# Last two attention units of the second batch split by ACT and DVE, and the fourth feed-forward chunk in pieces between the last tiles

## The reference

```python
x = hidden                                    # (2, 1024, 512)
n = layernorm(x)
q, k, v = n @ q_w.T + q_b, n @ k_w.T + k_b, n @ v_w.T + v_b      # 16 heads of 32
attn = softmax(causal(q @ k.T / sqrt(32))) @ v
x = x + layernorm(attn @ o_w.T + o_b)
h = silu(layernorm(x) @ w_gate.T) * (layernorm(x) @ w_up.T)      # 2048 wide
x = x + layernorm(h @ w_down.T)
```

## Time and profile before

| | |
|---|---|
| median of 3 runs | 1028.7 us (1028.31 to 1029.04) |
| the profiled execution, its own time | 1027.8 us |
| its span from first to last instruction | 1026.0 us |
| mean granted clock of TensorE | 0.986 of full speed |
| busy: PE, DVE, POOL, ACT | 980.4, 720.4, 691.2, 410.4 us |
| start and projections of the first batch | 0 to about 85 us |
| units 14 and 15 | 444.7 to 471.4 and 471.4 to 500.1 us |
| residual of the second batch | 500 to 554.4 us |

### The profile page before, as it was taken

The page is one execution under the profiler, slowest core; times in us unless marked ns, Lnnn a source line. Parts: engine busy times, 40 slices in busy tenths (PEclk is TensorE's granted clock), DMA queues, the critical chain, the costliest instruction groups (busy, mean ns, idle before and its releaser), DMA issues.

```text
span 1026.0 us, 15720 instructions
## 1 busy us (share of the span) xinstructions
PE 980.4 (96%) x5669; PEld 754.7 (74%) x5669; DVE 720.4 (70%) x1418; ACT 410.4 (40%) x717; POOL 691.2 (67%) x498
## 2 busy tenths in 40 slices
PE   5998999999999999998898999999999999999997
PEld 4766676766776776755576888888888888888886
DVE  6676777887597777875778577776665877777722
ACT  4215455555215555554335233332543433333232
POOL 4204888799535999999266976653688768776273
PEclk8999999999999999999899999999999999999999
DMA  6232333323421333231132222111432322211043
GB/s 224 78 88 58 96 83 89 87 76 78 134 82 35 93 88 89 73 95 42 62 112 96 93 76 77 62 62 44 161 113 93 112 77 74 98 62 62 20 154 134
DMA packets 49182, 90.70 MB, mean 88 GB/s; under 512 B 10448, under 2 KB 10960, under 8 KB 48848
## 3 DMA queue, kind: packets, MB, share of 16 engines
q1 hardware_dynamic: 48560, 89.43, 28.7%
q10 hardware_dynamic: 544, 0.26, 0.1%
HBM read 55.84 MB, written 8.39 MB: 63 GB/s over the span
## 4 chain that ended last, share of the span: by engine, by line
PE 75%; DVE 11%; POOL 7%; ACT 2%; issue 2%; DMA 2%; SPq 1%; POOLq 0%; ACTq 0%; DVEq 0%
PE ps L1649 19%; PE ps L1651 18%; PE ps L1650 18%; PE ps L1744 6%; PE ps L1715 5%; PE ps L1778 5%; POOL p_sum L747 3%; PE ps L1792 1%; DVE p_sum L1268 1%; DVE xt_lo L1282 1%; DMA x_in<-x 1%; POOL p_sum L743 1%; POOL p_sum L740 1%; DVE stats L1444 1%; PE ps L1752 1%
## 5 line engine op out<-in xcount | busy, mean ns | idle before, releaser
L1305 DVE CUSTOM_DVE_ANT_0 ps<-ps,mask_q 128x384 f32<-128x384 f32 (+7 forms) x256 | 189.9, 780 | 67.9 <-PE ps L1715 65.0
L1744 PE MATMUL ps<-q_stack,k_stack 98*128 98x512 f32 (+3 forms) x384 | 117.0, 382 | 9.4 <-ACT p_own L982 3.3
L1715 PE MATMUL ps<-k_stack,q_stack 96*128 96x512 f32 (+3 forms) x384 | 108.9, 364 | 1.6 <-DVE m_full L1305 0.9
L769 POOL TENSOR_TENSOR dn_lo<-dn_raw,dn_hi 128x512 fp32r<-128x512 f32 x48 | 65.7, 1370 | 47.2 <-ACT dn_hi L1074 47.2
L1744 PEld LDWEIGHTS ps<-q_stack,k_stack 98*128 98x128 f32 x384 | 62.7, 192 | 33.7 <-ACT p_own L982 8.3
L1715 PEld LDWEIGHTS ps<-k_stack,q_stack 96*128 96x128 f32 x384 | 66.6, 192 | 27.1 <-DVE m_full L1305 11.4
L814 POOL TENSOR_TENSOR gu_lo<-s_raw,gu_hi 128x1024 fp32r<-128x1024 f32 x27 | 64.8, 2402 | 23.2 <-ACT gu_hi L1145 23.2
L982 ACT ACTIVATE p_own<-ps 128x512 f32<-128x512 f32 x112 | 61.0, 598 | 42.8 <-PE ps L1744 23.7
L982 ACT ACTIVATE x_in<-ps 128x512 f32<-128x512 f32 x112 | 60.9, 598 | 36.5 <-PE ps L1744 20.4
L1168 ACT ACTIVATE silu<-ps 128x512 f32<-128x512 f32 x27 | 16.2, 599 | 141.5 <-DVE ps L1540 141.5
L810 POOL TENSOR_TENSOR a_lo<-gu_raw,a_hi 128x512 fp32r<-128x512 f32 x27 | 35.8, 1327 | 51.8 <-ACT a_hi L1138 51.7
(11 more groups left out here) (224 smaller groups left out, 2827.8 us busy)
## 6 DMA issues: line engine op xcount, KB each, us to landing
gu_raw<-gu_w SPq DMA_DIRECT2D x37, 512.0 KB, 3.6
dn_raw<-dn_w SPq DMA_DIRECT2D x48, 256.0 KB, 2.6
x_in<-x SPq DMA_DIRECT2D x32, 256.0 KB, 4.4
q_stack<-st_hi SPq DMA_DIRECT2D x128, 64.0 KB, 2.0
k_stack<-st_hi SPq DMA_DIRECT2D x128, 64.0 KB, 2.0
qk_raw<-qk_w SPq DMA_DIRECT2D x16, 256.0 KB, 3.0
q_stack<-st_lo SPq DMA_DIRECT2D x64, 64.0 KB, 2.0
k_stack<-st_lo SPq DMA_DIRECT2D x64, 64.0 KB, 2.0
```

The source lines that it names most:

```text
L769: nc.gpsimd.tensor_tensor(dn_lo[:, s], dn_raw[:, s], dn_hi[:, s].bitcast(F32), ALU.subtract).then_inc(dn_split, 1)
L1305: nc.vector.tensor_tensor_reduce(out=scores, in0=scores, in1=mask_q[:, SEQ - (t + 1) * P:], scale=1.0, scalar=MASKED, op0=ALU.add, op1=ALU ...
L1715: last = nc.tensor.matmul(bank[:, 0:width], q_stack[0:QK_ROWS, s, h, t * P:(t + 1) * P], k_stack[0:QK_ROWS, s, h, half * CH:half * CH + wi ...
L1744: last = nc.tensor.matmul(bank[:, at_col:at_col + n * P], k_stack[0:ROWS, s, h, kt * P:(kt + 1) * P], q_stack[0:ROWS, s, h, t * P:(t + n) ...
```

## The change

Units 14 and 15: quarters 0, 1 and 2 of `attn` are rounded by ACT between the rounds of unit 14 (after rounds 0, 4 and 6) and their rests are taken by DVE, quarter 0 in unit 14 before its last four maxima, quarters 1 and 2 in unit 15 before the adds. POOL's three splits go; its eighth token step moves behind the second residual tile. DVE's adds of unit 15 begin before `normalise(14)`, which stands between the third and the fourth. PE does the late products of the unit before first, then four unread products, the transposed maxima, and five (unit 14) or ten (unit 15) more. Start: seven unread products instead of four before tiles 1 to 7. Residual: chunk 3 is cut into its gate part after T 5, and halves of its up part after T 6 and T 7; there are no unread products before T 6 and three before T 7. ACT rounds tile 6 earlier and puts tile 7 between the two silus; DVE's `hidden(0)` comes before tile 7's rest. `down(0)` waits bank by bank, behind ten unread products.

```diff
-BUSY_AT_TILE = {**{_t: 4 for _t in range(1, TT)}, 13: 6, 2 * TT + 14: 8, 2 * TT + 15: 8}
+BUSY_AT_TILE = {**{_t: 7 for _t in range(1, TT)}, 13: 6, 2 * TT + 15: 3}
+HI_OF_PARTS = (0, 4, 6)
-AFTER_TILE = {("O", 3): 1, ("T", 4): 2, ("T", TT - 1): 3}
+WHOLE = ((0, 0, KT), (1, 0, KT))
+AFTER_TILE = {("O", 3): (1, WHOLE), ("T", 4): (2, WHOLE), ("T", 5): (3, ((0, 0, KT),)), ("T", 6): (3, ((1, 0, KT // 2),)),
+              ("T", 7): (3, ((1, KT // 2, KT),))}
@@ POOL, units @@
-                    if u >= UNITS - 2:
+                    if b + 1 < BATCH and u >= UNITS - 2:
                         pool.wait_ge(late_full, late_of((b + 1) * UNITS - 1, 1))
                         split_attn(b, u - (UNITS - 2))
                     if g + 1 == ALL_UNITS:
                         gu_rest(0)
                         gu_rest(1)
-                        of_tokens(T_STEPS - 1)
...
-                split_attn(b, KT - 2)
+                if b + 1 < BATCH:
+                    split_attn(b, KT - 2)
@@ POOL, residual tiles @@
+                    if b + 1 == BATCH and t == 1:
+                        of_tokens(T_STEPS - 1)
@@ ACT @@
+            def hi_of_part(b, k):
+
+                act.wait_ge(late_full, late_of((b + 1) * UNITS - 1, 1))
+                act.wait_ge(bank_free, use_of_sums(b * UNITS + 2 * k + 1) + 2)
+                nc.scalar.activation(xt_hi[:, b, k, :], attn[:, k, :], ACT.Copy).then_inc(attn_part_hi, 1)
...
+                    if g + 2 == ALL_UNITS and r in HI_OF_PARTS:
+                        hi_of_part(BATCH - 1, HI_OF_PARTS.index(r))
...
-                    if t >= lag:
+                    if t >= lag and (b + 1 < BATCH or t <= TT):
                         hi_of_xt(b, t - lag, use_of("T", b, t - lag))
+                    if b + 1 == BATCH and t == TT:
+                        hi_of_xt(b, t + 1 - lag, use_of("T", b, t + 1 - lag))
...
-                    for n in range(PARKED):
-                        silus(n)
+                    silus(0)
+                    hi_of_xt(BATCH - 1, TT - 1, use_of("T", BATCH - 1, TT - 1))
+                    silus(1)
@@ DVE @@
-            def add_up(g):
+            def add_up(g, between):
...
+                between()
                 vec.wait_ge(p_ready, scored(g, 4, 1))
...
+            def lo_of_part(b, k):
+
+                vec.wait_ge(attn_part_hi, k + 1)
+                nc.vector.tensor_tensor(xt_lo[:, b, k, :], attn[:, k, :], xt_hi[:, b, k, :].bitcast(F32), ALU.subtract).then_inc(attn_split, 1)
...
                 max_rows(g)
+                if not ahead:
+                    for k in range(1, KT - 1):
+                        lo_of_part(BATCH - 1, k)
...
-                if has_sums(g):
+                if not ahead:
+                    vec.wait_ge(bank_full, use_of_sums(g - 1) + SUM_BANKS)
+                    add_up(g, lambda: normalise(g - 1, None))
+                elif has_sums(g):
                     normalise(g - 1, None)
-                if not ahead:
-                    add_up(g)
                 if ahead:
                     maxima(g + 1, range(EARLY, len(MAXES) - 4))
+                if ahead and not projected:
+                    lo_of_part(BATCH - 1, 0)
...
+                    if b + 1 == BATCH and t == TT + 2:
+                        hidden(0)
                     if t >= lag:
                         lo_of_xt(b, t - lag, use_of("T", b, t - lag))
+                    if b + 1 == BATCH and t == TT + 2:
+                        hidden(1)
...
-                    if b + 1 == BATCH and t > TT:
-                        hidden(t - TT - 1)
@@ PE @@
-                if g + 2 == ALL_UNITS + 1 and n == EARLY:
-                    keep_busy(LATE_BANK, 5)
+                if g + 1 == ALL_UNITS and n == EARLY:
+                    keep_busy(LATE_BANK, 4)
...
             def transpose_maxima(g):
 
-                if g + 2 >= ALL_UNITS:
-                    pe.wait_ge(late_free, late_of(ALL_UNITS - 1, 1))
-                    keep_busy(LATE_BANK, 10)
...
-                transpose_maxima(g)
+                if projected:
+                    transpose_maxima(g)
                 if has_sums(g):
                     values(g - 1, LATE_VALUES)
+                if not projected:
+                    pe.wait_ge(late_free, late_of(ALL_UNITS - 1, 1))
+                    keep_busy(LATE_BANK, 4)
+                    transpose_maxima(g)
+                    keep_busy(LATE_BANK, 10 if g + 1 == ALL_UNITS else 5)
...
-            def gate_and_up(n):
+            def gate_and_up(n, pieces=WHOLE):
...
-                for part, bank in enumerate((0, 2) if blk else (G_BANK, U_BANK)):
+                for part, k0, k1 in pieces:
+                    bank = (0, 2)[part] if blk else (G_BANK, U_BANK)[part]
...
-                    last.then_inc(gu_full, 1)
+                    if k1 == KT:
+                        last.then_inc(gu_full, 1)
@@ PE, down @@
+                if n == 0:
+                    pe.wait_ge(bank_free, USES - (USES - 1 - banks[0]) % RING)
+                    keep_busy(banks[0], 10)
...
                 for t in range(BT):
+                    if n == 0:
+                        pe.wait_ge(bank_free, USES - (USES - 1 - banks[t]) % RING)
...
-            pe.wait_ge(bank_free, USES)
             down(0, first=True)
```

More of the change, by code:

```diff
@@ L451, in build @@
         attn_last_split = sem("attn_last_split")
+        attn_part_hi = sem("attn_part_hi")
         var_ready = sem("var_ready")
@@ L1853, in residual @@
                     extra(kind, t)
-            def gate_and_up(n):
-                s, k = n % 2, plain_of(n)
+            def gate_and_up(n, pieces=WHOLE):
+                s = n % 2
                 blk = n // CHUNKS
@@ L1865, in gate_and_up @@
                     pe.wait_ge(parked if early else h_ready, 2 * (n - 1) if early else n - 1)
-                for part, bank in enumerate((0, 2) if blk else (G_BANK, U_BANK)):
+                for part, k0, k1 in pieces:
+                    bank = (0, 2)[part] if blk else (G_BANK, U_BANK)[part]
                     if n == 0 and part:
                         pe.wait_ge(acc_read, ALL_UNITS)
-                    for k in range(KT):
+                    for k in range(k0, k1):
                         w = slice(k * GU + part * P, k * GU + (part + 1) * P)
                         last = three(ps[:, bank + s], gu_hi[:, s, w], gu_lo[:, s, w], xt_hi[:, 0, k, cols], xt_lo[:, 0, k, cols], k == 0, k == KT - 1)
-                    last.then_inc(gu_full, 1)
+                    if k1 == KT:
+                        last.then_inc(gu_full, 1)
             def down(n, first=False, final=False):
                 m, banks = down_of(n), OUT_BANKS[down_of(n) // CHUNKS]
+                if n == 0:
+                    pe.wait_ge(bank_free, USES - (USES - 1 - banks[0]) % RING)
+                    keep_busy(banks[0], 10)
                 pe.wait_ge(h_ready, n + 1)
@@ L1963, in first_chunks @@
                 if (kind, t) in AFTER_TILE:
-                    gate_and_up(AFTER_TILE[kind, t])
+                    gate_and_up(*AFTER_TILE[kind, t])
             pe.wait_ge(consts_made, 1)
```

## The result

| | before | after |
|---|---|---|
| median, lowest and highest run | 1028.3 us (1027.03 to 1029.04, 5 runs) | 1022.25 us (1020.45 to 1025.09, 5 runs) |
| the profiled execution, time and span | 1027.8, 1026.0 us | 1022.25, 1020.5 us |
| mean granted clock | 0.986 | 0.988 |

The account below looks back on a forecast made before the run. PE was taken as the bound (75% of the last chain), waiting at the start, in units 14 and 15 and at the residual's end. -1.2 - 3.0 - 2.0 = -6.2 on 1027.8 gave 1021.6, as median 1022.5; range 1018.8 to 1026.6 us.

Parts of the forecast that it names:

- Start: Before the first projection: three more unread products before seven tiles keep the clock up, -1.2 us, bounds -1.7 and +0.7.
- the idle stretch covers tiles 6 and 7: Start: tiles 6 and 7, late by up to 0.7 together, are covered by PE's 2.17 us wait before the projection.
- the clock of the start stays down: Rival, start: DVE still ends a wait before the projection, so the clock stays low; 1023.7 us, 25%.
- Units 14 and 15: Unit term: the matrix of ones of unit 15 starts at 496.1 instead of 499.12, -3.0 us, bounds -6.5 and -0.5.
- up to 3.7 on POOL: Unit 14: DVE's three subtractions of 1.23 us each fall on POOL's adds and delay POOL by up to 3.7 us.
- the third step: Unit 15, DVE: after the copy and the add of 768 columns, the 0.42 us add, done at 484.8.
- The lock and not the halving: Unit 15: POOL and DVE exclude each other for a whole instruction; with halved speeds the sum would be -8.6.
- The rival of 12%: Unit 15: PE becomes the bound at 1.2 GHz from the scores on; ones near 498.6, time 1025.0 us, 12%.
- the slower one: Rival, unit 14: PE waits for the maxima's DMA, the clock falls near 450 and stays at 1.2 GHz; 1031 us, 8%.
- Residual: End of the residual: `down(0)` 2.5 us earlier, `down(1)` moved by -2.3 or -1.0; term taken as -2.0 us.
- about 1: Residual, `hidden(0)`: allowance in us for POOL's four sums of a pair standing in DVE's way.
- -2.3 and -1.0: Residual: shift of `down(1)` in us, the first if `hidden(1)` precedes POOL's weight rest, the second if the rest cuts in.

Follow-up runs that it names:

- `residual_only`: Kernel before with only the residual part (chunk 3 in pieces, unread products of tiles 6 and 7, silus and hidden around tile 7, bank-wise `down(0)`): 1025.07 us, ratio 0.9973.
- `start_only`: Kernel before with seven instead of four unread products before tiles 1 to 7 and nothing else of the change: 1029.73 us, ratio 1.0017.
- `units_only`: Only the changes of units 14 and 15, with start and residual as in the kernel before: 1023.39 us, ratio 0.9959.
- `tokens_in_15`: Changed kernel with four unread products at the start and POOL's token step put back into unit 15: 1022.99 us, ratio 0.9946.
- `maxima_first`: Changed kernel with four unread products at the start and PE's order in units 14 and 15 as before (one unread product less): 1019.64 us, ratio 0.9915.
- `start4_fill0`: Changed kernel with four unread products at the start and twelve before the first scores of unit 0: 1020.18 us, ratio 0.9927.
- `combined`: Changed kernel with four unread products at the start, twelve before unit 0's first scores, and PE's old order in units 14 and 15: 1021.26 us, ratio 0.993.
- `after_again`: The changed kernel, unaltered, run once more as a control: 1022.9 us, ratio 0.9951.
- `after_start4`: Changed kernel with four instead of seven unread products before tiles 1 to 7: 1020.95 us, ratio 0.9934.

## Why the prediction was right, and where it was not

**Start: the term failed, in sign.** It rested on three statements. That three more products lift the clock of 34 to 38.3 was seen (1.00 in 4 of 4 profiles with seven), but it was 1.00 in 8 of 10 with four too: the 0.60 of the earlier trace rows belonged to that execution more than to the program. In the two profiles with 0.60 and 0.61 (the kernel before and `residual_only`) PE was idle for 2.17 and 2.09 before the projection, in the twelve others for 1.41 to 1.68, so the reason given, a shorter wait, fits; but the wait is mostly short with four as well. That the idle stretch covers tiles 6 and 7 was wrong beyond some 0.8 us. DVE's rest of tile 7, before and in `start_only`:

```profile
33.08 0.67 DVE L1282 TENSOR_TENSOR xt_lo<-ps,xt_hi 128x512 fp32r<-128x512 f32 x1
```
```profile
33.68 0.69 DVE L1282 TENSOR_TENSOR xt_lo<-ps,xt_hi 128x512 fp32r<-128x512 f32 x1 [0.29 <-ACT xt_hi L936]
```

Before, DVE came to it without a wait, from other work. In `start_only` it waited for ACT's rounding of that same tile, so the wait of PE begins with the tile, moves with it and keeps its 1.41. The first maxima are at 82.57 in `start_only`, 82.34 in `units_only`. Last, nothing was said of unit 0, which is 50 us further on and lost its clock. The loss (1.7 by `start_only`, 1.9 in the profile of after) lies outside the stated bounds of -1.7 and +0.7. A quarter of the chance lay on "the clock of the start stays down"; what happened is neither that nor the forecast.

**Units 14 and 15: right in mechanism, 1.3 short.** The times of after less the 1.91 by which unit 0 was late can be laid beside the steps. `add_up(14)` began at 453.95 (forecast 454) and ended at 476.5 (forecast 477 to 478). It is the term "up to 3.7 on POOL" that was mis-sized: `add_up(14)` ran 22.5 us, before 20.4, so the three subtractions held POOL up by 2.1. DVE lost more in these meetings (3.1) than POOL did. From there every step has its forecast length: both rests to 482.1 (forecast 483.4), the third step to 483.6 (484.8), `normalise` to 486.7 (488.1), the ones at 494.85 (496.1). The total of 14 was not through at 479.3 but at 479.8, because PE took 1.9 for it at 1.2 GHz; that was covered by POOL's rests, which the copy met anyway (2.40).

**The lock and not the halving**: right, on the copy, the 768 columns of `tokens_in_15` and its 2.5 us.

**PE is not the bound of unit 15**: right. At 494 to 499 the clock was 1.00 and the ones start 0.15 after the last add. The rival of 12% is out. So is the slower one: PE idled 1.45 before the first scores of unit 14, where it had not idled before, and 1.50 before those of unit 15, more than the 0.74 before. But at 450 to 457, the rival's deciding point, the clock was 1.00; the stretch from 461 was at 0.50, as before the change, and from 483.5 to 499 it was 1.00. `maxima_first`, `start4_fill0` and `combined` show that the placement itself neither gains nor loses.

**Residual: right in mechanism, 1.1 short.** With the 2.36 added by which the ones were sooner, `hidden(0)` began at 548.96 (forecast 548.9), its `h_lo` was done at 551.3 (551.8), `hidden(1)` began at 551.8 (552.5) and was done at 554.5 (555.5). The allowance of "about 1" for POOL's sums was 0.5, and the weight rest, which decided between -2.3 and -1.0, did not cut in. The -3.1 lies beyond even the nearer of the two: `hidden(1)` began 0.7 and ended 1.0 sooner than forecast. In `after_again` the rest did cut in. `down(0)` stood 52.25 behind the ones (forecast 52.8), and `down(1)` came 3.23 behind it, not 3.6 to 4.9.

So two terms gained 1.3 and 1.1 more than forecast, and the first came out 3.1 worse than forecast. That these nearly cancel is luck.

## What to carry to other kernels

- A stretch at low clock in one profile is a price only if the same stretch is low in a second execution of the same code; look at that before paying for unread products, and look for the next wait without cover behind them. Check the clock column against the time from one product to the next.
- An idle stretch covers a delay only when what ends it does not itself start with the delayed work.
- Where PE and DVE both come late to where they meet, the cure of either side shows nothing alone; ask for each which engine would be waited for next.

## What was not expected of the hardware

- The granted clock of identical code differs between executions. In 34 to 38.3 us, with four, the kernel before had 0.60 and began 13 products, `units_only` had 1.00 and 20 products. The runs of the changed kernel spread over 4.6 and 5.5 us, the kernel before over 2.0 to 4.8.
- The column of the granted clock can say 1.00 where PE runs at 1.2 GHz. `units_only`, a stretch and four unread products inside it, then the same four at full clock:

```profile
14.00:18.00 4.00, 3.38 (x15) 2.54 (x16) 3.39 (x8) 3.35 (x5) 1.69 (x1) 1.00 0.52 146
```
```profile
15.14 1.06 PE L1681 MATMUL ps<-mask_q,ident_bf 128*128 128x256 bf16 x4
...
28.13 0.61 PE L1681 MATMUL ps<-mask_q,ident_bf 128*128 128x256 bf16 x4
```

  The same holds for `after_start4`: in both, products of 512 columns begin 0.43 us apart up to about 26 us and 0.23 apart later. In neither did this slow start delay the first maxima (82.34 and 82.25, before 83.50).
- An idle stretch of 1.3 to 1.6 us before the first scores of unit 0 was followed by 1.2 GHz for several microseconds in some executions and by 2.4 GHz in others. Why the seven products at the start, some 50 us earlier, make that likelier stays open: no run separates their effect on the clock from the small shift of all that follows.
- A difference of 0.9 us in when POOL's rest and DVE's last step begin, one against the other, went with 3.7 us at the end of the residual in the one execution that had it: PE got a wait of 1.80, where it was 0.21, and then the lower clock.
